# State-space stage of a decoder layer: loops written out, units beyond the last and the empty first accumulation left out

## The chip, the cores and the metric

The kernel runs on one core of one Trainium2 chip. The metric is device microseconds of that core, from launch to end; the lower the better. The five engines (TensorE or PE, VectorE or DVE, ScalarE or ACT, GpSimd or POOL, SyncE or SP) each run their own instruction stream and meet at semaphores.

## The reference, cut to what matters

One decoder layer on x of 16 x 128 x 256: a state-space mixer, then cross attention, then a feed-forward network, each followed by a residual and a layer norm. The change touches the mixer alone:

```python
H, P, N, G, K, CH, E = (32, 128, 128, 8, 4, 32, 256)
proj = x @ in_proj_w.T
gate, hbc, dt = split(proj)
hbc = silu(causal_conv4(hbc) + conv_b)
hs, B, C = split(hbc)                 # B, C: 8 groups, shared by 4 heads each
X = hs.reshape(b, s, H, P) * dt[..., None]
A_cum = cumsum(-exp(A_log) * dt)
y[l] = sum_{m<=l} (C_l . B_m) exp(A_cum_l - A_cum_m) X_m + D * hs_l
h = y * silu(gate)
h = h * rsqrt(mean over 512 channels of h*h + EPS)     # per group of 4 heads
out = (norm_w * h) @ out_proj_w.T
x = layernorm(x + out)
```

## The kernel before

The function decoder_layer calls five stages one after the other, each in a block of its own with a barrier at its end: front (projections of B, C and dt, the products gs of C and B, the cumulative sums), state_space, middle, attention, output. All of them but state_space are plain instruction streams without loops.

The stage state_space works in units of one head and 512 tokens (4 sequences). Four heads that share a norm make a round; four rounds (one for each quarter of the tokens) use the same weight group; there are 8 groups, 32 rounds, 128 units. The stage is a software pipeline written out by hand: in slot m every engine does one part of the units m+3, m+2, m+1 and m.

- PE: x_ps of unit m+3 (L446, project: 6 matmuls of 512 columns), d_ps (L463, L465) and the transpose t_ps (L471) of m+2, y_ps (L481) and gate_ps (L446) of m+1, the output o_ps (L494) of m, and behind a round's last unit the sums of squares ss_ps (L500).
- ACT: first tap of the convolution from x_ps (L525), the exponentials decay (L535), silu of xs (L541), silu of the gate (L547). Exponential and silu each load their table, so two table loads stand in each slot.
- DVE: the other three taps (L603, each waits for the one before), xdt (L611), y (L619), mix (L625).
- POOL: hid = y times the silu of the gate (L659), its square (L666) and the running sum (L670).

At the start of a round's first slot DVE runs finish: var from ss_ps (L585), POOL raises it to the power -0.5 (L649), and four scaled additions bring o_ps into acc (L590). In the slots of each group's last round ACT rounds the next group's weights (L516, w_hi), and DVE scales the output weights (L573, wo) and makes the low part (L576, w_lo). x_ps, gate_ps, t_ps, d_ps, y_ps and o_ps have one buffer each.

Three slots lead in (slot(-1, ...), with Python numbers). The rest are loops on each engine's sequencer: PE and POOL loop over 32 rounds, ACT and DVE over 8 groups with an inner loop of 3 rounds, SP over 8 groups. Heads, tokens and semaphore values are computed in registers; each wait whose value comes from a register is put on an increment of a semaphore named held that nothing waits for. Since the loop bodies are all alike, three things are computed that nobody uses:

- finish(0) adds o_ps and ss_ps, cleared by memsets, before there is anything in them (out_unit and out_used count it);
- the last three slots also work on the units 128, 129 and 130;
- the last round rounds the weights of a ninth group, and SP loads the first group again for it.

Of the kernel before, what the change touches and what calls it, by code (L numbers as in the profile page):

```python
# [17 lines left out]
P = 128  # L18
# [331 lines left out]
def state_space(nc, mem, io):  # L350
# [5 lines left out]


    held = mem["held"]
    xh, xl, gs, cw, cb, dt, ncum, cumT, onehot, mask, acc, dpar, ident, identb = (
        mem[k] for k in ("xh", "xl", "gs", "cw", "cb", "dt", "ncum", "cumT", "onehot", "mask", "acc", "dpar",  # L360
                         "ident", "identb"))
# [8 lines left out]
    def head_of(r, h):  # L370
        return (r // TG) % G * HG + h

    with ExitStack() as ctx:
# [6 lines left out]
        def sem(name):  # L380
            return ctx.enter_context(nc.semaphore(name))

# [17 lines left out]
        x_ps = ps("x_ps", [P, BG, SEQ])  # L400
# [8 lines left out]
        (hi_ready, w_ready, consts, x_ready, tap_ready, chain, conv_done, xs_ready,  # L409
         gate_ready, sg_ready, t_ready, xdt_ready, d_ready, decay_ready, mix_ready, y_ready, yd_ready, hid_ready,  # L410
         sq_ready, sq_chain, out_unit, out_used, var_ready, rms_ready) = (
            sem("ss_" + n) for n in
            ("hi_ready", "w_ready", "consts", "x_ready", "tap_ready", "chain",
             "conv_done", "xs_ready", "gate_ready", "sg_ready", "t_ready", "xdt_ready", "d_ready", "decay_ready",
             "mix_ready", "y_ready", "yd_ready", "hid_ready", "sq_ready", "sq_chain", "out_unit", "out_used", "var_ready",
# [4 lines left out]
        @block.sync  # L420
        def _(sp):
            def load(g):
                cols = bass.ds(g * (HG * P), HG * P)
                for to, of in ((w_raw[:, 0, :, :], io["winT"][:, bass.ds(g * (HG * P) + OFF_X, HG * P)]
                                .rearrange("(k p) c -> p k c", p=P)),
                               (w_raw[:, 1, :, :], io["winT"][:, cols].rearrange("(k p) c -> p k c", p=P)),
                               (wo_raw[:, :, :], io["woutT"][cols, :].rearrange("(h p) e -> p h e", p=P))):
                    sp.dma_start(to, of).then_inc(w_loaded, 16)

            with sp.Fori(0, G) as g:  # L430
                sp.wait_ge(w_ready, g * HG + HG)
                load((g + 1) % G)

        @block.tensor
        def _(pe):
            pe.sem_inc(out_unit, 1)
            pe.wait_ge(consts, 4)

            def project(to, i, n, r, h, ready):

                tok = bass.ds(r % TG * GT, GT)
                pe.wait_ge(w_ready, r // TG * HG + (h + 1))
                pe.sem_inc(held, 1)
                for k in range(KE):
                    for s, (w, x) in enumerate(((w_hi, xh), (w_hi, xl), (w_lo, xh))):
                        mm = pe.matmul(to[:, :, :], w[:, i, k, h * P:(h + 1) * P], x[:, k, tok],  # L446
                                       start=(k == 0 and s == 0), stop=(k == KE - 1 and s == 2))
                mm.then_inc(ready, 1)

            def slot(it, hh, primed):  # L450

                n, r, h = unit(it, hh, 3)
                if primed or n > 0:
                    pe.wait_ge(conv_done, n)
                project(x_ps, 0, n, r, h, x_ready)

                n, r, h = unit(it, hh, 2)
                if primed or n >= 0:

                    if primed or n > 0:  # L460
                        pe.wait_ge(decay_ready, n)
                        pe.sem_inc(held, 1)
                    pe.matmul(d_ps[:, :, :], onehot[:, bass.ds(head_of(r, h), 1), :],  # L463
                              cumT[:, bass.ds(r % TG * GT, GT)], start=True, stop=False)
                    pe.matmul(d_ps[:, :, :], identb[:, :], mask[:, :], start=False, stop=True).then_inc(d_ready, 1)  # L465

                    if primed or n > 0:
                        pe.wait_ge(xdt_ready, n)
# [5 lines left out]
                n, r, h = unit(it, hh, 1)  # L474
                if primed or n >= 0:
                    if primed or n > 0:
                        pe.wait_ge(yd_ready, n)
                    pe.wait_ge(xdt_ready, n + 1)
                    pe.wait_ge(mix_ready, n + 1)
                    for b in range(BG):  # L480
                        mm = pe.matmul(y_ps[:, b, :], xdt[:, h % 2, b, :], mix[:, h % 2, b, :],  # L481
                                       start=True, stop=True)
                    mm.then_inc(y_ready, 1)
                    if primed or n > 0:
                        pe.wait_ge(sg_ready, n)
                    project(gate_ps, 1, n, r, h, gate_ready)

                if primed:
                    n, r, h = unit(it, hh, 0)
                    pe.wait_ge(hid_ready, n + 1)  # L490
                    if h == 0:
                        pe.wait_ge(out_used, it + 1)
                    for b in range(BG):
                        mm = pe.matmul(o_ps[:, b, :], hid[:, h % 2, b, :],  # L494
                                  wo[:, bass.ds(r // TG % 2, 1), h, :].rearrange("p a e -> p (a e)"),
                                  start=(h == 0 and b % 2 == 0), stop=(h == HG - 1), skip_group_check=True)
                    if h == HG - 1:
                        pe.wait_ge(sq_ready, it * HG + HG)
# [3 lines left out]
                    mm.then_inc(out_unit, 1)  # L502

            for hh in range(HG - LEAD, HG):
                slot(-1, hh, False)
            with pe.Fori(0, ROUNDS) as it:
                for hh in range(HG):
                    slot(it, hh, True)

        @block.scalar  # L510
        def _(act):
            def round_weights(g, h):
                act.wait_ge(w_loaded, (g + 1) * (16 * LOADS))
                act.sem_inc(held, 1)
# [4 lines left out]
            def slot(it, hh, primed):  # L519
                n, r, h = unit(it, hh, 3)  # L520
                head = bass.ds(head_of(r, h), 1)

                act.wait_ge(x_ready, n + 1)
                act.sem_inc(held, 1)
                act.activation(xs[:, h, :, :], x_ps[:, :, :], ACT.Identity, bias=cb[:, head],  # L525
                               scale=cw[:, head, TAPS - 1]).then_inc(tap_ready, 1)

                n, r, h = unit(it, hh, 2)
                if primed or n >= 0:
                    if primed or n > 1:  # L530
                        act.wait_ge(mix_ready, n - 1)
                    act.wait_ge(d_ready, n + 1)
                    act.sem_inc(held, 1)
                    for b in range(BG):
                        ex = act.activation(decay[:, h % 2, b, :], d_ps[:, b, :], ACT.Exp,  # L535
                                            bias=ncum[:, bass.ds(r % TG * BG + b, 1), bass.ds(head_of(r, h), 1)])
                    ex.then_inc(decay_ready, 1)

                n, r, h = unit(it, hh, 3)
                act.wait_ge(conv_done, n + 1)  # L540
                act.activation(xs[:, h, :, :], xs[:, h, :, :], ACT.Silu).then_inc(xs_ready, 1)  # L541

                n, r, h = unit(it, hh, 1)
                if primed or n >= 0:

                    act.wait_ge(gate_ready, n + 1)
                    act.activation(sg[:, h % 2, :, :], gate_ps[:, :, :], ACT.Silu).then_inc(sg_ready, 1)  # L547

            for h in range(HG):
                round_weights(0, h)  # L550
            for hh in range(HG - LEAD, HG):
                slot(-1, hh, False)
            with act.Fori(0, G) as g:
                with act.Fori(0, TG - 1) as tg:
                    for hh in range(HG):
                        slot(g * TG + tg, hh, True)
                for hh in range(HG):
                    round_weights(g + 1, hh)
                    slot(g * TG + (TG - 1), hh, True)

        @block.vector
        def _(dve):
            dve.memset(ones[:, :], 1.0).then_inc(consts, 1)
            dve.memset(half[:, :], -0.5).then_inc(consts, 1)
            dve.memset(o_ps[:, :, :], 0.0).then_inc(consts, 1)
            dve.memset(ss_ps[:, :], 0.0).then_inc(consts, 1)
            dve.wait_ge(nw_loaded, 16)

            def rest_of_weights(g, h):
                dve.wait_ge(hi_ready, g * HG + (h + 1))  # L570
                dve.sem_inc(held, 1)

                dve.tensor_tensor(wo[:, bass.ds(g % 2, 1), h, :], wo_raw[:, h:h + 1, :],  # L573
                                  nw[:, bass.ds(g % G * HG + h, 1)].unsqueeze(2).to_broadcast([P, 1, E]), ALU.mult)
# [6 lines left out]
            def finish(it):  # L581

                dve.wait_ge(out_unit, it * HG + 1)
                dve.sem_inc(held, 1)
                dve.tensor_scalar(var[:, :], ss_ps[:, 0:BG], 1.0 / (HG * P), RMS_EPS,  # L585
                                  ALU.mult, ALU.add).then_inc(var_ready, 1)
                dve.wait_ge(rms_ready, it + 1)
                for b in range(BG):
                    to = acc[:, bass.ds((it + (TG - 1)) % TG * BG + b, 1), :].rearrange("p b e -> p (b e)")
# [3 lines left out]
            def slot(it, hh, primed):  # L593
                if primed and hh == 0:
                    finish(it)
                n, r, h = unit(it, hh, 3)
                head = bass.ds(head_of(r, h), 1)
                dve.wait_ge(tap_ready, n + 1)
                for s in range(1, TAPS):
                    if s > 1:  # L600
                        dve.wait_ge(chain, n * 2 + (s - 1))
                    to = xs[:, h, :, s:]
# [1062 lines left out]
```

## Time and profile before

| what | value |
|---|---|
| median of 3 runs | 2147.5 us (2147.41 to 2147.55) |
| profiled execution | 2146.56 us |
| its span, first to last instruction | 2144.8 us |
| PE busy | 1803.8 us, 84% |
| ACT busy | 1665.4 us, 78% |
| DVE busy | 1649.4 us, 77% |
| POOL busy | 580.7 us, 27% |
| mean granted TensorE clock | 0.978 |

Span and busy times are of one profiled execution; the median is of runs without a profile. The stage state_space fills the stretch from about 177 to 1076 us. Matmuls overlap, so that their busy time is no measure of idle time between them: the start times of the weight loads (PEld) say more.

### The profile page before, as it was taken

What the parts mean: (1) busy time and instruction counts of PE and PEld (TensorE: products, weight loads), DVE (VectorE), ACT (ScalarE), POOL (GpSimd) and SP (SyncE); (2) the same over time, 40 slices, a digit from 0 to 9 for tenths busy, and PEclk for the clock granted to TensorE, in tenths of its full rate; (3) what the DMA queues carried; (4) which work ended last, traced back from release to release, by engine and by line L of the source; (5) the groups of instructions that cost most, each with busy time, mean ns of one, the idle gap of its engine ahead of it and who ended that gap; (6) DMA issues with size and microseconds to landing.
All of it is one profiled execution on the core that took longest, in us unless ns stands there. A gap on an engine that the chain in (4) does not pass through costs nothing. (4 is left out here: it accounts for less than half of the span.)

```text
span 2144.8 us, 37991 instructions
## 1 busy us (share of the span) xinstructions
PE 1803.8 (84%) x12364; PEld 1273.8 (59%) x12514; DVE 1649.4 (77%) x2759; ACT 1665.4 (78%) x2987; POOL 580.7 (27%) x482
## 2 busy tenths in 40 slices
PE   6987999999999999999967677777777777774999
PEld 4775878787878787878746333333333333333887
DVE  5886686767686767676888699999999999994443
ACT  4666888888888888888826899999999999994211
POOL 2001555555555555555510000100000100003000
PEclk8998999999999999999989999999999999997999
DMA  4000000000000000000082499999999999995000
GB/s 139 16 6 30 0 30 0 29 0 29 0 29 0 29 0 29 0 26 4 0 182 39 78 182 183 185 184 184 180 185 185 183 183 180 186 186 122 11 11 20
DMA packets 566249, 173.94 MB, mean 81 GB/s; under 512 B 535168, under 2 KB 558592, under 8 KB 566144
## 3 DMA queue, kind: packets, MB, share of 16 engines
q1 hardware_dynamic: 566144, 172.57, 42.8%
q8 instruction: 63, 1.03, 0.2%
q14 instruction: 42, 0.34, 0.1%
HBM read 27.83 MB, written 2.10 MB: 14 GB/s over the span
## 5 line engine op out<-in xcount | busy, mean ns | idle before, releaser
L1223 ACT ACTIVATE levels<-s_ps,nb,qstep 128x512 int16<-128x512 f32 (+1 forms) x768 | 695.8, 915 | 32.7 <-DVE nb L1188 31.7
L1178 DVE TENSOR_REDUCE mx<-s_ps 128x1 f32<-128x512 f32 (+1 forms) x768 | 630.8, 862 | 26.4 <-PE s_ps L1128 26.4
L1128 PE MATMUL s_ps<-kT,qT 128*128 128x512 bf16 x1447 | 445.6, 386 | 200.1 <-ACT levels L1223 181.2
L603 DVE SCALAR_TENSOR_TENSOR xs<-x_ps,cw,xs 128x508 f32<-128x508 f32 (+2 forms) x393 | 291.2, 741 | 174.3 <-ACT xs L525 135.9
L1128 PEld LDWEIGHTS s_ps<-kT,qT 128*128 128x128 bf16 x1532 | 107.8, 97 | 434.8 <-ACT levels L1223 383.7
L659 POOL TENSOR_TENSOR hid<-y,sg 128x512 f32<-128x512 f32 x128 | 175.2, 1369 | 277.7 <-ACT sg L547 185.1
L494 PE MATMUL o_ps<-wo,hid 128*128 x1024 | 242.8, 380 | 4.9 <-DVE acc L590 4.9
L494 PEld LDWEIGHTS o_ps<-wo,hid 128*128 128x128 f32 x1024 | 192.7, 189 | 39.5 <-issue 9.8
L525 ACT ACTIVATE xs<-x_ps,cb,cw 128x512 f32<-128x512 f32 x131 | 101.9, 777 | 116.1 <-PE x_ps L446 116.1
L1246 POOL TENSOR_TENSOR sum_part<-sums 128x16 f32<-128x16 f32 x16 | 3.4, 211 | 689.5 <-ACT levels L1223 689.5
L1136 PEld LDWEIGHTS ao_ps<-vi,levels_T 128*128 128x128 f16 x4096 | 139.9, 96 | 66.9 <-DMA levels_T<-levels 7.6
L535 ACT ACT_TABLE_LOAD x130 | 166.8, 1283 | 2.4
L541 ACT ACT_TABLE_LOAD x130 | 166.8, 1283 | 2.3
L1223 ACT ACTIVATION_READ_ACCUMULATOR levels<-s_ps,nb,qstep 128x1 f32 x768 | 150.6, 196 | 0.0
L535 ACT ACTIVATE decay<-d_ps,ncum 128x128 f32<-128x128 f32 x520 | 148.7, 369 | 1.6
L446 PE MATMUL x_ps<-xh,w_hi 128*128 (+1 forms) x262 | 121.5, 464 | 30.6 <-DVE xs L603 25.7
L1136 PE MATMUL ao_ps<-vi,levels_T 128*128 128x16 f16 x4096 | 140.4, 169 | 7.2 <-DMA levels_T<-levels 7.2
L309 DVE SCALAR_TENSOR_TENSOR bc<-raw_ps,cw,bc 128x1016 f32<-128x1016 f32 (+2 forms) x96 | 119.9, 1265 | 29.9 <-ACT bc L234 27.7
L481 PE MATMUL y_ps<-mix,xdt 128*128 128x128 f32 x1032 | 136.3, 275 | 0.0
L670 POOL TENSOR_TENSOR ssum<-ssum,sq 128x512 f32<-128x512 f32 x96 | 131.3, 1368 | 7.5
L481 PEld LDWEIGHTS y_ps<-mix,xdt 128*128 128x128 f32 x1032 | 125.4, 192 | 0.0
L446 PE MATMUL gate_ps<-xh,w_hi 128*128 (+1 forms) x258 | 112.1, 434 | 0.0
(201 smaller groups left out, 3255.2 us busy)
## 6 DMA issues: line engine op xcount, KB each, us to landing
w_raw<-winT_dram SPq DMA_DIRECT2D x18, 512.0 KB, 4.5
wo_raw<-woutT_dram SPq DMA_DIRECT2D x9, 512.0 KB, 5.7
kT<-zeros SPq DMA_DIRECT2D x4, 1024.0 KB, 18.7
qT<-zeros SPq DMA_DIRECT2D x4, 1024.0 KB, 16.1
levels_T<-levels SPq DMA_TRANSPOSE x256, 4.6
acc<-xT_dram SPq DMA_DIRECT2D x4, 512.0 KB, 5.5
w_bc<-winT_dram SPq DMA_DIRECT2D x16, 128.0 KB, 2.4
acc<-x_dram SPq DMA_DIRECT2D x1, 2048.0 KB, 11.1
```

What stands on the lines that cost most here:

```text
L446: mm = pe.matmul(to[:, :, :], w[:, i, k, h * P:(h + 1) * P], x[:, k, tok], start=(k == 0 and s == 0), stop=(k == KE - 1 and s == 2))
L481: mm = pe.matmul(y_ps[:, b, :], xdt[:, h % 2, b, :], mix[:, h % 2, b, :], start=True, stop=True)
L494: mm = pe.matmul(o_ps[:, b, :], hid[:, h % 2, b, :], wo[:, bass.ds(r // TG % 2, 1), h, :].rearrange("p a e -> p (a e)"), start=(h == 0 and ...
L535: ex = act.activation(decay[:, h % 2, b, :], d_ps[:, b, :], ACT.Exp, bias=ncum[:, bass.ds(r % TG * BG + b, 1), bass.ds(head_of(r, h), 1)])
L541: act.activation(xs[:, h, :, :], xs[:, h, :, :], ACT.Silu).then_inc(xs_ready, 1)
L603: dve.scalar_tensor_tensor(to, x_ps[:, :, 0:SEQ - s], cw[:, head, TAPS - 1 - s], to, ALU.mult, ALU.add).then_inc(chain if s < TAPS - 1 els ...
L659: pool.tensor_tensor(hid[:, hh % 2, :, :], y[:, hh % 2, :, :], sg[:, hh % 2, :, :], ALU.mult).then_inc(hid_ready, 1)
L670: pool.tensor_tensor(ssum[:, :, :], ssum[:, :, :], sq[:, :, :], ALU.add).then_inc(sq_ready, 1)
L1128: return pe.matmul(s_ps[:, BANKS[h % 2][chunk], :], qT[:, qt, h, :], kT[:, h, at:at + GT], start=True, stop=True)
L1136: mm = pe.matmul(o_ps[:, h * HD:(h + 1) * HD], lT[:, s, j, :].bitcast(F16), vi[:, j, h * HD:(h + 1) * HD], start=(j == 0), stop=(j == T // ...
L1178: dve.tensor_reduce(mx[:, u, at:at + 1], src, AX.XY if what == "cd" else AX.X, ALU.max).then_inc(max_done, 1)
L1223: act.activation(levels[:, s, at:at + banks * GT].rearrange("p (c k) -> p c k", c=banks), s_ps[:, bank:bank + banks, :], ACT.Exp, bias=nb[ ...
```

## The change

The loops of state_space become Python loops: each engine has all its instructions one after the other, with constants for heads, tokens and semaphore values, and without held. The slot number m runs from -3 to 127 on PE, ACT and DVE, and a part is written only if its unit lies in 0 to 127. The finish of a round r runs from r = 0, at the start of the next round; the last one behind the last slot. The empty one, the two memsets of o_ps and ss_ps, the ninth group's weights and the reload are gone. The order of each engine's instructions within a slot is as before. x_ps gets a first axis of length 1; buffers are chosen by n % 2 for h % 2, which is the same.

```diff
-    def unit(it, hh, ahead):
-        r = it + (hh + ahead) // HG
-        return r * HG + (hh + ahead) % HG, r, (hh + ahead) % HG
+    UNITS = ROUNDS * HG
+    def place(n):
+        r, h = divmod(n, HG)
+        g, tg = divmod(r, TG)
+        return r, h, g, tg, g * HG + h
...
-            with sp.Fori(0, G) as g:
-                sp.wait_ge(w_ready, g * HG + HG)
-                load((g + 1) % G)
+            for g in range(1, G):
+                load(g)
...
-            pe.sem_inc(out_unit, 1)
-            pe.wait_ge(consts, 4)
...
-                pe.wait_ge(w_ready, r // TG * HG + (h + 1))
-                pe.sem_inc(held, 1)
+                pe.wait_ge(w_ready, head + 1)
...
-            for hh in range(HG - LEAD, HG):
-                slot(-1, hh, False)
-            with pe.Fori(0, ROUNDS) as it:
-                for hh in range(HG):
-                    slot(it, hh, True)
+            for m in range(-LEAD, UNITS):
+                n = m + 3
+                if n < UNITS:
+                    if n >= 1:
+                        pe.wait_ge(conv_done, n - 1 + 1)
+                    project(x_ps[:, n % 1, :, :], 0, n, x_ready)
...
-                    if h == 0:
-                        pe.wait_ge(out_used, it + 1)
+                    if h == 0 and r:
+                        pe.wait_ge(out_used, r)
...
+            for m in range(-LEAD, UNITS):
+                if m >= 0 and m // HG % TG == TG - 1 and m // (HG * TG) + 1 < G:
+                    round_weights(m // (HG * TG) + 1, m % HG)
...
-            dve.memset(o_ps[:, :, :], 0.0).then_inc(consts, 1)
-            dve.memset(ss_ps[:, :], 0.0).then_inc(consts, 1)
...
+                if m > 0 and m % HG == 0:
+                    if m == HG:
+                        dve.wait_ge(acc_loaded, 16)
+                        dve.wait_ge(consts, 2)
+                    finish(m // HG - 1)
...
+            finish(ROUNDS - 1)
...
-            pool.wait_ge(consts, 4)
-            with pool.Fori(0, ROUNDS) as it:
-                factor(it)
+            pool.wait_ge(consts, 2)
+            for n in range(UNITS):
+                r, h, g, tg, head = place(n)
+                if h == 0 and r:
+                    factor(r - 1)
```

## Rows read from the trace of the kernel before

**Rows 1.** Windows: body and tail; busy us (x count) per engine, PE clock, DMA.
```profile
199.00:1041.80 842.80, 815.44 (x4402) 664.95 (x4464) 623.01 (x958) 710.79 (x1147) 456.47 (x372) 1.00 0.04 13
1041.80:1075.80 34.00, 27.09 (x144) 21.37 (x145) 28.87 (x43) 24.89 (x41) 17.44 (x13) 1.00 0.00 0
```
**Rows 2.** Windows: an ordinary round, then a weight group's last round.
```profile
553.40:579.50 26.10, 25.99 (x144) 21.47 (x145) 18.02 (x30) 22.38 (x37) 14.07 (x12) 1.00 0.00 0
605.60:635.35 29.75, 27.13 (x144) 21.40 (x147) 25.81 (x36) 24.23 (x40) 16.44 (x12) 1.00 0.05 13
```
**Rows 3.** Timeline (start, duration in us) of PE's weight loads, ordinary round.
```profile
546.30 0.19 PEld L446 LDWEIGHTS x_ps<-xl,w_hi 128*128 128x128 f32 x1
...
553.48 0.19 PEld L446 LDWEIGHTS x_ps<-xl,w_hi 128*128 128x128 f32 x1
...
559.87 0.19 PEld L446 LDWEIGHTS x_ps<-xl,w_hi 128*128 128x128 f32 x1
...
566.15 0.19 PEld L446 LDWEIGHTS x_ps<-xl,w_hi 128*128 128x128 f32 x1
```
**Rows 4.** Timeline of PE's weight loads, group's last round and after.
```profile
605.76 0.19 PEld L446 LDWEIGHTS x_ps<-xl,w_hi 128*128 128x128 f32 x1
...
611.08 1.59 PEld L494 LDWEIGHTS o_ps<-wo,hid 128*128 128x128 f32 x8 [1.04 <-issue]
...
613.91 0.19 PEld L446 LDWEIGHTS x_ps<-xl,w_hi 128*128 128x128 f32 x1
...
642.79 0.19 PEld L446 LDWEIGHTS x_ps<-xl,w_hi 128*128 128x128 f32 x1
```
**Rows 5.** Timeline of DVE, same round ([idle before <- releaser]).
```profile
609.24 1.66 DVE L590 SCALAR_TENSOR_TENSOR acc<-o_ps,rms,acc 128x256 f32<-128x256 f32 x4 [1.13 <-POOL rms L649]
...
611.72 1.62 DVE L603 SCALAR_TENSOR_TENSOR xs<-x_ps,cw,xs 128x504 f32<-128x504 f32 x2 [0.16 <-DVE xs L603]
613.25 0.68 DVE L611 TENSOR_TENSOR xdt<-t_ps,dt 128x512 f32<-128x512 f32 x1
...
620.40 0.68 DVE L611 TENSOR_TENSOR xdt<-t_ps,dt 128x512 f32<-128x512 f32 x1
```
**Rows 6.** Lines L573, L576, L659: count, min/median/max ns, first and last start.
```profile
L573 DVE TENSOR_TENSOR wo<-wo_raw,norm_w x36: 407/1320/1348, 178.6 to 1065.8; 128x256 f32 x32, 128x256 f32<-128x256 f32 x4
...
L576 DVE TENSOR_TENSOR w_lo<-w_raw,w_hi x36: 679/1522/1525, 179.0 to 1067.0; 128x512 fp32r<-128x512 f32 x36
...
L659 POOL TENSOR_TENSOR hid<-y,sg x128: 1262/1274/1660, 201.4 to 1065.1; 128x512 f32<-128x512 f32 x128
```
**Rows 7.** Timeline, head of the stage; last row from an ordinary round.
```profile
177.29 0.91 DVE L565 MEMSET o_ps<- 128x1024 f32 x1 [0.21 <-issue]
...
178.97 0.68 DVE L576 TENSOR_TENSOR w_lo<-w_raw,w_hi 128x512 fp32r<-128x512 f32 x1
...
179.72 0.29 PEld L446 LDWEIGHTS x_ps<-xh,w_hi 128*128 128x128 f32 x1 [3.89 <-issue]
...
183.58 2.29 DVE L603 SCALAR_TENSOR_TENSOR xs<-x_ps,cw,xs 128x508 f32<-128x508 f32 x3 [1.12 <-ACT xs L525]
...
201.69 1.66 DVE L590 SCALAR_TENSOR_TENSOR acc<-o_ps,rms,acc 128x256 f32 x4 [1.33 <-POOL rms L649]
...
562.80 2.51 DVE L603 SCALAR_TENSOR_TENSOR xs<-x_ps,cw,xs 128x508 f32<-128x508 f32 x3 [1.66 <-ACT xs L525]
```
**Rows 8.** Timeline, tail of the stage.
```profile
1066.80 1.28 ACT L535 ACT_TABLE_LOAD   x1
...
1068.10 1.15 ACT L535 ACTIVATE decay<-d_ps,ncum 128x128 f32<-128x128 f32 x4
...
1074.11 1.66 DVE L590 SCALAR_TENSOR_TENSOR acc<-o_ps,rms,acc 128x256 f32<-128x256 f32 x4 [1.13 <-POOL rms L649]
```
**Rows 9.** Page: a DMA queue; a costliest group (busy, mean ns, idle before, releaser).
```profile
q8 instruction: 63, 1.03, 0.2%
...
L1223 ACT ACTIVATE levels<-s_ps,nb,qstep 128x512 int16<-128x512 f32 (+1 forms) x768 | 695.8, 915 | 32.7 <-DVE nb L1188 31.7
```

More of the change, by code:

```diff
@@ L399, in state_space @@
         rms = sb("rms", [P, BG])
[L400 removed]
+        x_ps = ps("x_ps", [P, 1, BG, SEQ])
         gate_ps = ps("gate_ps", [P, BG, SEQ])
@@ L517, in round_weights @@
                          w_raw[:, :, :, cols].rearrange("p i k c -> p (i k) c")).then_inc(hi_ready, 1)
[L519 to L530, printed above, removed]
+            for h in range(HG):
+                round_weights(0, h)
@@ new lines, in _ @@
+            for m in range(-LEAD, UNITS):
+                if m >= 0 and m // HG % TG == TG - 1 and m // (HG * TG) + 1 < G:
+                    round_weights(m // (HG * TG) + 1, m % HG)
+                n = m + 3
+                if n < UNITS:
+                    r, h, g, tg, head = place(n)
+                    act.wait_ge(x_ready, n + 1)
+                    act.activation(xs[:, h, :, :], x_ps[:, n % 1, :, :], ACT.Identity, bias=cb[:, head:head + 1],
+                                   scale=cw[:, head, TAPS - 1:TAPS]).then_inc(tap_ready, 1)
+                n = m + 2
+                if 0 <= n < UNITS:
+                    r, h, g, tg, head = place(n)
+                    if n > 1:
@@ L531, in slot @@
                         act.wait_ge(mix_ready, n - 1)
                     act.wait_ge(d_ready, n + 1)
-                    act.sem_inc(held, 1)
                     for b in range(BG):
-                        ex = act.activation(decay[:, h % 2, b, :], d_ps[:, b, :], ACT.Exp,
-                                            bias=ncum[:, bass.ds(r % TG * BG + b, 1), bass.ds(head_of(r, h), 1)])
+                        ex = act.activation(decay[:, n % 2, b, :], d_ps[:, b, :], ACT.Exp,
+                                            bias=ncum[:, tg * BG + b, head:head + 1])
@@ L551, in _ @@
[L551 to L559, printed above, removed]
+                n = m + 3
+                if n < UNITS:
+                    act.wait_ge(conv_done, n + 1)
+                    act.activation(xs[:, n % HG, :, :], xs[:, n % HG, :, :], ACT.Silu).then_inc(xs_ready, 1)
@@ L588, in finish @@
                 for b in range(BG):
-                    to = acc[:, bass.ds((it + (TG - 1)) % TG * BG + b, 1), :].rearrange("p b e -> p (b e)")
+                    to = acc[:, r % TG * BG + b, :]
                     ins = dve.scalar_tensor_tensor(to, o_ps[:, b, :], rms[:, b:b + 1], to, ALU.mult, ALU.add)
                 ins.then_inc(out_used, 1)
[L593 to L602, printed above, removed]
-                    dve.scalar_tensor_tensor(to, x_ps[:, :, 0:SEQ - s], cw[:, head, TAPS - 1 - s], to,
-                                             ALU.mult, ALU.add).then_inc(chain if s < TAPS - 1 else conv_done, 1)
-                n, r, h = unit(it, hh, 2)
-                if primed or n >= 0:
-                    if primed or n > 1:
+            dve.memset(ones[:, :], 1.0).then_inc(consts, 1)
@@ new lines, in _ @@
+            dve.memset(half[:, :], -0.5).then_inc(consts, 1)
+            dve.wait_ge(nw_loaded, 16)
+            for h in range(HG):
+                rest_of_weights(0, h)
+            for m in range(-LEAD, UNITS):
+                if m >= 0 and m // HG % TG == TG - 1 and m // (HG * TG) + 1 < G:
+                    rest_of_weights(m // (HG * TG) + 1, m % HG)
+                if m > 0 and m % HG == 0:
[3 more added lines that the diff above has]
+                    finish(m // HG - 1)
+                n = m + 3
+                if n < UNITS:
+                    r, h, g, tg, head = place(n)
+                    dve.wait_ge(tap_ready, n + 1)
+                    for s in range(1, TAPS):
+                        if s > 1:
+                            dve.wait_ge(conv_chain, n * 2 + (s - 1))
+                        to = xs[:, h, :, s:]
+                        dve.scalar_tensor_tensor(to, x_ps[:, n % 1, :, 0:SEQ - s], cw[:, head, TAPS - 1 - s:TAPS - s], to,
+                                                 ALU.mult, ALU.add).then_inc(conv_chain if s < TAPS - 1 else conv_done, 1)
+                n = m + 2
+                if 0 <= n < UNITS:
+                    r, h, g, tg, head = place(n)
+                    if n > 1:
```

178 lines of the change are left out of this document (72 added, 106 removed).

## The prediction

> **What bounds the kernel now.** I read the windows view first. The state-space stage runs from about 177 us to 1076 us, and in its body TensorE is busy 815 of 843 us, at full clock [rows 1]. An ordinary round keeps PE busy 25.99 of 26.10 us while DVE has 18.02; in the last round of a weight group PE has 27.13 of 29.75 and DVE 25.81 [rows 2]. So there are two regimes. Then I read the weight loads in order of time. The second load of x_ps in each slot marks where one slot hands the array to the next. The slots of an ordinary round last 7.18, 6.39 and 6.28 us [rows 3] and again about 6.29: 6.285 is the array's own time, the 7.18 holds the 8 pairs of ss_ps (0.89), and only the 6.39 has 0.11 of idle. Saturated, a round costs 4 x 6.285 + 0.89 = 26.03 us, and no loop, branch or register operation can be seen in it.
>
> Around a weight group's last round it is different: from 605.76 to 642.79, five slots, 37.03 us [rows 4] against 5 x 6.285 + 0.89 = 32.3. There DVE sets the pace: from xdt at 613.25 to the next at 620.40 is 7.15 us of unbroken DVE work [rows 5], because the weights' L573 and L576 take 1.32 and 1.52 us beside POOL, where they can take 0.41 and 0.68 [rows 6]. The excess of the body adds up: 842.8 - 31 x 26.03 = 36 us, of which 7 groups x 4.7 = 33, some 1.8 in ordinary rounds and 1 in the first.
>
> **Head.** Removed are the memsets of o_ps and ss_ps (0.91 and 0.48, from 177.29), ahead of the first weights [rows 7]. L573 could then start when the first w_hi is cast, at about 177.65, for 178.65 now: 1.0 us on the path to the first x_ps. The dropped held increments give about 0.1 in each of three hops, 0.3, and the entry into the loops 0.5 (the third lead slot lasts 6.74, for 6.27 before it). The empty finish (var, POOL's power, four adds, ending 1.66 after 201.69 [rows 7]) holds DVE for 3.1 us ahead of the fourth convolution; PE's slot is 7.23 and would be 6.285: 0.95. Sum 2.75 us.
>
> **Ordinary rounds.** PE's instruction stream is the same, so only the 0.11 goes, in the middle rounds, 16 of them: 1.8 us. The branch, the register operations and held increments are hidden by the queue of matmuls; were that cover gone they would show as the 0.47 below.
>
> **Group-last rounds.** Register operations sit between a wait and the instruction that needed it. The three taps take 2.51 us in the loop and 2.29 where the code is already plain, in the head [rows 7]: 0.22 a slot on DVE. From the end of the taps (611.72 + 1.62 = 613.34) to PE's next x_ps (613.81, a tenth before the row at 613.91) is 0.47 us; in the head, 178.97 + 0.68 = 179.65 to 179.72 is 0.07 [rows 4, 5, 7]. So 0.4 for such a hop. POOL to DVE: 1.33 of waiting for a 1.02 power, where 1.13 is possible when DVE's registers are done ahead [rows 5, 7]: 0.2. The first slot, 8.15 [rows 4], loses two hops (w_hi to L573, taps to x_ps) and the tap gaps: 7.13. Its o_ps, which today waits until 611.08 for the adds that end at 610.90 [rows 4, 5], moves with them. The next two run at 7.15 - 0.22 = 6.93 each. The fourth and fifth together follow DVE through the finish: 6.93, and then 7.15 less the weights' 2.7 plus the finish's 3.0, which is 7.4, less 0.42, 7.0. Sum 7.13 + 6.93 + 6.93 + 13.9 = 34.9 for 37.03, 2.1 to 2.3 us a group, 16 us over 7 groups. What is late next is the same DVE chain, not PE. The bounds: 0 if DVE stays tied to POOL (an L576 of 1.52 ends when POOL lets it), 33 if DVE stops binding; I take the gaps alone, since L573's earlier start meets a hid that takes up to 1.66 for 1.27 [rows 6] and ends no sooner.
>
> **Tail.** From the start of the last round's first slot (1041.8) to the last add (1075.8) are 34.0 us, with PE busy 27.1 [rows 1]. Removed: the whole weights work of that round (DVE and ACT again), x_ps of three units (3 x 1.38), d_ps and t_ps of two, y_ps and gate_ps of one, about 8.6 us of PE, and a reload by SP's queue that nobody waits for. What remains is a chain. With an ordinary first slot (t = 0 at its start) PE is through at 6.3; t_ps of the last unit waits for its silu (6.9); y_ps of unit 126 waits for mix (7.3) and ends at 8.3, gate_ps at 9.7, o_ps at 11.4. ACT loads a table and does four exponentials (1.28 + 1.15 [rows 8]), until 9.8, loads again for the silu of 126: 11.7. Then y_ps and gate_ps of the last unit: 13.7; silu 14.5. POOL works in order: hid(126) 13.0, its square 14.05, its sum 15.35, hid(127) 16.65, square 17.7, sum 19.0. ss_ps after it ends at 19.95, var 20.3, power 21.4, adds (1.66 [rows 8]) 23.1. So 34.0 - 23.2 = 10.8 us. Bounds: 12.5 if ACT's silu of unit 126 needs no table load behind the exponentials; 3 if most of the removed work hides beside this chain (rival d below). I take 10.8, since each link of the chain has a duration in rows of this stage.
>
> **Sum.** 2.75 + 1.8 + 16 + 10.8 = 31.4 us. The profiled execution took 2146.56 us (span 2144.8 and 1.8 around it); it becomes 2115.2, and against the median of 2147.5, 2116. The later stages begin behind a barrier with their own loads and only shift.
>
> **Where straight-line code costs.** The plain program is longer: 68 rows a slot on PE, so some 33 more blocks of 256 on PE's instruction queue and about 28 on the other engines'. Now there are 63 packets on q8, 1.03 MB [rows 9], for 24878 weight loads and matmuls: 97 blocks if each were fetched each time, so the loop's are not fetched again, and its branch costs PE nothing [rows 3]. In the attention stage, plain code with denser rows and busy DMA, ACT's 768 activations at L1223 waited 32.7 us in all, 31.7 of it for DVE [rows 9]: at most 1.0 us is left for fetching.
>
> The Trainium skill (Runtime: NRT & Kernel Launch, Instruction fetch mechanics) says that straight code is fetched ahead and mostly hidden, and that a taken branch out of the two-block window stalls until its block is fetched. On the first point the attention rows agree. By the second the loops' back edges would cost now and their removal bring more than my sum; the 63 packets and the saturated slots around the back edge say that these loops stay in the window.
>
> **Rivals.**
> (a) DVE stays bound to POOL in the group-last rounds and nothing of the 16 comes: 2147.5 - 15.4 = 2132. For it: L576's median is more than twice its shortest time [rows 6]. Against: the tap gaps lie where POOL doesn't matter. 0.13.
> (b) Without register operations the DVE chain meets POOL in a better phase and the weights' operations shorten by 0.7 us a slot: the slots fall to PE's 6.285, all 33 us come, and the time is 2147.5 - 2.75 - 1.8 - 33 - 10.8 = 2099. For it: both have been as short as 0.41 and 0.68 [rows 6]. Against: POOL's three operations need 3.6 to 4.4 us of each slot, so they nearly always meet. 0.09.
> (c) Slower: code supply. Each of some 61 new blocks stalls its engine. Price: q8's 0.2% of 16 engines' span for 63 packets is about 1.1 us a packet [rows 9], so 61 x 1.1 = 67, and 2116 + 67 = 2183. It decides from 0.5 us a block (31.4 / 61). Against: the attention rows. 0.05.
> (d) The tail's work was hidden: it saves 3 instead of 10.8, 2124. It speaks for it that the chain through ACT and POOL remains; against, that in the last slots PE, DVE and ACT all have rows of units that don't exist. 0.08.
>
> **How the numbers follow.** The forecast as such, 2106 to 2126, has 0.65. The range takes in (d) and nearly (a): 2105 to 2131; out of it are (b), (c) and part of (a). A change under 0.2% (4.3 us) can't be told from none. Faster: all but (c) and a remainder of (c)'s small stalls that eat just the gain: 0.93; within 0.2%: 0.02; slower: 0.05.
>
> **What would show it.** DVE's first L576 ending near 178.7; no L590 before the second round; ordinary rounds of 26.0 to 26.1 between x_ps marks; group-last slots of 6.9 us with three taps in 2.3; from the last round's start to the last add about 23 us, with PE waiting for POOL's hid in the last slot; q8 near 96 packets with no gap beside them. Ordinary rounds that lengthen by more than 0.1, or idle time of PE without a releaser, would make it wrong.

## The result, and the profile after

The changed kernel takes 2116.13 us (median of 5 runs, 2112.38 to 2120.53) against 2147.41 us before (5 runs, 2143.91 to 2147.55): ratio 0.9863, 95% interval 0.9845 to 0.9882. The forecast was 2116.0.

I measure the state-space stage from VectorE's memset of ones to the end of its last add to acc. It took 898.79 us (176.98 to 1075.77) and takes 865.12 (177.65 to 1042.77): 33.7 less. The profiled execution as a whole got only 27.0 shorter (2119.57 for 2146.56), so some 6.7 were given back outside this stage (0.7 ahead of it, 6.0 behind); more on that below. I cut the stage at the marks of the prediction, the second x_ps weight load of each slot:

```
                        before    after   change   forecast
first mark               2.91     1.90    -1.0     -1.0
lead (3 slots)          19.24    16.91    -2.3     -0.8
body (31 rounds)       842.82   823.02   -19.8     -18.75
tail                    33.84    23.29   -10.5     -10.8
five slots at a group's end (of the body, 7 times)
                        37.03    34.57   -2.5      -2.1 to -2.3
```

First the windows view of the changed kernel (start:end, length, then busy time and count of PE, PEld, DVE, ACT and POOL, PE's clock, DMA share, GB/s): the body and the tail, which answer to [rows 1], then an ordinary round and a weight group's last round, which answer to [rows 2].

```profile
199.00:1019.40 820.40, 809.84 (x4393) 664.42 (x4453) 622.03 (x950) 708.89 (x1144) 455.81 (x371) 1.00 0.04 12
1019.40:1042.80 23.40, 18.44 (x101) 15.06 (x101) 10.51 (x20) 10.66 (x18) 15.44 (x13) 1.00 0.00 1
...
567.89:593.93 26.04, 25.93 (x144) 21.59 (x146) 18.05 (x29) 22.43 (x38) 14.15 (x12) 1.00 0.00 1
593.93:621.82 27.89, 26.88 (x144) 21.27 (x145) 25.86 (x35) 23.79 (x40) 16.39 (x12) 1.00 0.05 12
```

PE's idle time in the body fell from 27.4 us (842.80 - 815.44) to 10.6. The ordinary round is 26.04 long, the 26.03 of a saturated array. The group's last round went from 29.75 to 27.89 with the same DVE work in it, 25.86: DVE still sets the pace there. The weight loads of PE and DVE's timeline around that round (start, duration) answer to [rows 4, 5]:

```profile
593.93 0.19 PEld L438 LDWEIGHTS x_ps<-xl,w_hi 128*128 128x128 f32 x1
...
600.80 0.19 PEld L438 LDWEIGHTS x_ps<-xl,w_hi 128*128 128x128 f32 x1
...
607.72 0.19 PEld L438 LDWEIGHTS x_ps<-xl,w_hi 128*128 128x128 f32 x1
...
628.49 0.19 PEld L438 LDWEIGHTS x_ps<-xl,w_hi 128*128 128x128 f32 x1
```
```profile
594.54 0.42 DVE L537 TENSOR_TENSOR wo<-wo_raw,norm_w 128x256 f32<-128x256 f32 x1 [1.24 <-ACT w_hi L497]
594.88 0.68 DVE L540 TENSOR_TENSOR w_lo<-w_raw,w_hi 128x512 fp32r<-128x512 f32 x1
...
596.77 1.66 DVE L553 SCALAR_TENSOR_TENSOR acc<-o_ps,rms,acc 128x256 f32<-128x256 f32 x4 [1.13 <-POOL rms L610]
598.35 2.29 DVE L577 SCALAR_TENSOR_TENSOR xs<-x_ps,cw,xs 128x508 f32<-128x508 f32 x3
600.56 0.68 DVE L586 TENSOR_TENSOR xdt<-t_ps,dt 128x512 f32<-128x512 f32 x1
...
601.81 0.68 DVE L601 TENSOR_TENSOR mix<-decay,gs 128x512 f32<-128x512 f32 x1
602.41 1.49 DVE L537 TENSOR_TENSOR wo<-wo_raw,norm_w 128x256 f32<-128x256 f32 x1
603.83 1.52 DVE L540 TENSOR_TENSOR w_lo<-w_raw,w_hi 128x512 fp32r<-128x512 f32 x1
605.28 2.29 DVE L577 SCALAR_TENSOR_TENSOR xs<-x_ps,cw,xs 128x508 f32<-128x508 f32 x3
607.48 0.68 DVE L586 TENSOR_TENSOR xdt<-t_ps,dt 128x512 f32<-128x512 f32 x1
```

From 593.93 to 628.49 are 34.56 us in slots of 6.87, 6.92, 6.92, 7.18 and 6.67. The three taps now stand in one row of 2.29 us. They end at 600.64, and PE's next x_ps follows within 0.16 (mark 600.80); it was 0.57 before (613.34 to the mark at 613.91 [rows 4, 5]). From xdt to xdt DVE takes 6.92 us, still without a gap. The tail's timeline (ACT, POOL and the weight loads) has the chain of the prediction, with POOL near its end and PE waiting for it twice; it answers to [rows 8]:

```profile
1029.21 1.28 ACT L531 ACT_TABLE_LOAD   x1
...
1033.36 0.60 ACT L531 ACTIVATE sg<-gate_ps 128x512 f32<-128x512 f32 x1 [2.26 <-PE gate_ps L438]
...
1034.94 1.26 POOL L619 TENSOR_TENSOR hid<-y,sg 128x512 f32<-128x512 f32 x1
1036.26 1.59 PEld L483 LDWEIGHTS o_ps<-wo,hid 128*128 128x128 f32 x8 [1.61 <-POOL hid L619]
1036.29 1.04 POOL L627 TENSOR_TENSOR sq<-hid 128x512 f32<-128x512 f32 x1
1037.40 1.26 POOL L630 TENSOR_TENSOR ssum<-ssum,sq 128x512 f32<-128x512 f32 x1
...
1038.72 0.97 PEld L488 LDWEIGHTS ss_ps<-ones,ssum 128*128 128x128 f32 x8 [0.87 <-POOL ssum L630]
```

On the page, the queue of instructions and the attention stage's activations answer to [rows 9]:

```profile
q8 instruction: 100, 1.64, 0.3%
...
L1183 ACT ACTIVATE levels<-s_ps,nb,qstep 128x512 int16<-128x512 f32 (+1 forms) x768 | 695.6, 915 | 34.9 <-DVE nb L1148 34.9
```

### The profile page after: what moved, and what is told of

Read it like the earlier page. It is cut to its first block and busy times, and to the rows that moved or that the text cites. A ratio compares the mean times of both kernels' runs of the same rounds, so it can differ in the third digit from the quotient of the medians.

```text
span 2117.8 us, 33475 instructions
## 1 busy us (share of the span) xinstructions
PE 1796.3 (85%) x12321; PEld 1271.0 (60%) x12470; DVE 1629.6 (77%) x2730; ACT 1651.1 (78%) x2964; POOL 578.1 (27%) x481
## 5 line engine op out<-in xcount | busy, mean ns | idle before, releaser
L1183 ACT ACTIVATE levels<-s_ps,nb,qstep 128x512 int16<-128x512 f32 (+1 forms) x768 | 695.6, 915 | 34.9 <-DVE nb L1148 34.9
L577 DVE SCALAR_TENSOR_TENSOR xs<-x_ps,cw,xs 128x508 f32<-128x508 f32 (+2 forms) x384 | 284.6, 741 | 150.7 <-ACT xs L509 141.7
L483 PE MATMUL o_ps<-wo,hid 128*128 128x256 f32 x1024 | 242.3, 379 | 1.2 <-POOL hid L619 1.2
L1183 ACT ACTIVATION_READ_ACCUMULATOR levels<-s_ps,nb,qstep 128x1 f32 x768 | 150.6, 196 | 0.0
L438 PE MATMUL x_ps<-xh,w_hi 128*128 128x512 f32 x256 | 120.1, 469 | 14.6 <-DVE xs L577 10.4
L438 PE MATMUL gate_ps<-xh,w_hi 128*128 128x512 f32 x256 | 111.4, 435 | 0.0
```

Of the source, the lines that this page charges most:

```text
L438: mm = pe.matmul(to, w[:, i, k, h * P:(h + 1) * P], x[:, k, tg * GT:(tg + 1) * GT], start=(k == 0 and s == 0), stop=(k == KE - 1 and s == 2))
L483: mm = pe.matmul(o_ps[:, b, :], hid[:, n % 2, b, :], wo[:, g % 2, h, :], start=(h == 0 and b % 2 == 0), stop=(h == HG - 1), skip_group_che ...
L577: dve.scalar_tensor_tensor(to, x_ps[:, n % 1, :, 0:SEQ - s], cw[:, head, TAPS - 1 - s:TAPS - s], to, ALU.mult, ALU.add).then_inc(conv_chai ...
L1183: act.activation(levels[:, s, at:at + banks * GT].rearrange("p (c k) -> p c k", c=banks), s_ps[:, bank:bank + banks, :], ACT.Exp, bias=nb[ ...
```

## Experiments: the change in pieces

Four kernels were built from the kernel before, each with a part of the change; two more runs are of the changed kernel. All totals are medians of 4 or more runs; "stage" is the profiled execution's.

**Loops written out, nothing else** (`Fori` to `range` on all five engines, all work and the held increments kept):

```diff
-            with dve.Fori(0, G) as g:
-                with dve.Fori(0, TG - 1) as tg:
+            for g in range(G):
+                for tg in range(TG - 1):
-            with pe.Fori(0, ROUNDS) as it:
+            for it in range(ROUNDS):
```

> The kernel before with its loops written out, and nothing else: the increments of held, the memsets, the empty finish, the units 128 to 130 and the ninth weight group all stay. The stage lasted 898.8 us before and 865.1 after the change. My theory (in group-last rounds DVE sets the pace, and the register operations between a wait and its instruction cost 0.22 us a slot on DVE and 0.4 at each hop): the constants take most of it, held leaves about 0.1 a hop; stage 878 us, group-last middle slots 6.93. Rival (the gain is the waits sitting on held, not the registers): stage near 890, slots of 7.1.

Measured: 2123.15 us (2121.76 to 2129.96), ratio 0.9899 [0.9878, 0.9920]; stage 878.38, body 824.55, tail 32.37. The loops alone are 20.4 of the stage's 33.7 us. The held increments stay here, and the taps take 2.29 us all the same: it is the register operations between them that are gone. In the kernel before the source view of the taps' line has them on DVE's sequencer (count, then ns), and in this run it has none:

```profile
L603 DVEq FUSED_REGOPS  x384: 46/64/181, 202.2 to 1070.1; - x192
```

**The same, and no held increments** (`sem_inc(held, 1)` removed on PE, ACT and DVE):

> As the last one, and the increments of held are gone too, so that waits sit on the instructions themselves; all the unused work stays. My theory: stage 875.4 us (865.1 + 8.6 for the tail + 1.7 for memsets and empty finish), the five slots around a group's end 34.6 us as after the change. Rival (the removed work is what brought the gain in the body too): five slots stay near 37.

Measured: 2125.39 us (2125.05 to 2127.99), ratio 0.9903 [0.9886, 0.9919]; stage 876.86. The increments are worth 1.5 us of the stage; the totals can't tell that from nothing. They show in the first slot of a group's last round: 8.15 us before, 7.50 with only DVE's loops written out (below), 7.12 with all loops, 6.87 without the increments as well.

**Only DVE's loops written out** (and DVE's held increments gone):

> The kernel before with DVE's stream alone written out and its increments of held gone; PE, ACT, POOL and SP keep their loops and registers, all unused work stays. My theory: DVE's taps go from 2.51 to 2.29 and its slot in group-last rounds from 7.15 to 6.93; PE keeps its 0.47 behind the taps, so the five slots take about 35.3 instead of 37.0; stage 884 us. Rival (PE's or ACT's loop is what costs): stage 896 or more.

Measured: 2131.57 us (2126.92 to 2132.70), ratio 0.9920 [0.9903, 0.9937]; stage 882.20, body 827.64, a group's five slots 35.19. The windows view of its group-last round, against 29.75 in [rows 2] and 27.89 above:

```profile
598.88:627.16 28.28, 27.03 (x146) 21.29 (x145) 26.04 (x36) 24.18 (x41) 16.35 (x12) 1.00 0.05 11
```

One engine's loops and increments bring 16.6 us. The other four engines' loops and increments bring 5.3 more (882.20 - 876.86, the run before this one), mostly in the groups (35.19 to 34.55 each, 4.5 in all) and in the lead (0.9).

**Loops kept, tail cut** (last round peeled, units beyond the last not computed, no ninth weight group):

```diff
-            with pe.Fori(0, ROUNDS) as it:
+            with pe.Fori(0, ROUNDS - 1) as it:
                 for hh in range(HG):
                     slot(it, hh, True)
+            for hh in range(HG):
+                slot(ROUNDS - 1, hh, True, last=True)
```

> The kernel before with its loops, but the last round stands behind them without the units 128 to 130, without the ninth group's weights and the reload. Empty finish and memsets stay. My theory (tail 33.8 to 23.3 us after the change, little of it by constants): stage 888 us, tail 23.5. Rival (the cut work was hidden behind the chain through ACT and POOL, and it is the constants that shortened the tail): stage 896, tail 31.

Measured: 2136.17 us (2133.19 to 2137.99), ratio 0.9952 [0.9935, 0.9968]; stage 886.22, tail 23.50 for 33.84, body 840.67. The tail is its own 10.3 us, whatever the loops do. The body got 2.1 us shorter too, though its loops are kept: 0.3 us in each group's five slots. No run says why.

**The changed kernel again**, on the chip of the experiments below:

> The kernel of the change as it is, on the same chip as the next three, for a time beside theirs. It took 2116 us (2112.4 to 2120.5) before. In its profile the state-space stage was 33.7 us shorter, but all that follows took 6 us longer (middle stage 134.1 for 131.0, attention 738.8 for 736.8, output 202.1 for 201.2). If that is chance of where the clock's cold stretches fall, the stage is again 865.1 and the rest between 1066 and 1075; if the change itself causes it, the rest is 1075 again.

Measured: 2116.31 us (2114.83 to 2117.17), ratio 0.9860 [0.9845, 0.9875]; stage 866.06 with a lead of 18.19. The lead of 16.91 above is thus not the change's alone. The windows view of 178 to 198 us shows what differs, first the kernel before, then after, then this run:

```profile
178.00:198.00 20.00, 13.01 (x42) 9.05 (x44) 11.84 (x21) 10.34 (x18) 0.00 (x0) 0.57 0.25 79
```
```profile
178.00:198.00 20.00, 13.53 (x50) 9.08 (x52) 13.42 (x22) 12.93 (x22) 0.00 (x0) 0.83 0.24 79
```
```profile
178.00:198.00 20.00, 14.21 (x48) 9.95 (x49) 13.30 (x22) 12.79 (x22) 0.00 (x0) 0.74 0.23 79
```

The granted clock (third from the right) was 0.57, 0.83 and 0.74 of full speed there, means of stretches at half (1.2 GHz) and at full speed (2.4 GHz); in the kernel before PE had its half speed from 178.3 to 195.3 without a break. Two executions of the same program differ by 1.3 us in the lead with it.

**The head put back into the changed kernel**:

```diff
+            dve.memset(o_ps[:, :, :], 0.0).then_inc(consts, 1)
+            dve.memset(ss_ps[:, :], 0.0).then_inc(consts, 1)
...
-                if m > 0 and m % HG == 0:
+                if m >= 0 and m % HG == 0:
                     finish(m // HG - 1)
```

> The kernel after, with the head of the kernel before put back: VectorE clears o_ps and ss_ps (two memsets, 1.0 us), TensorE waits for all four memsets, and the empty first accumulation (1 us) runs before unit 0; all else stays straight code with the tail cut. My theory (head = 1.0 for the first weight load, then about 1 us for the empty accumulation in the first round): the stage grows from the 865.1 to 866.1 us of the changed kernel to 867 to 868, the first x_ps mark from 1.9 to 2.9 us, body and tail stay at 822.8 and 23.3; the whole about 2118. Rival 1 (the lead shrank for another reason, the clock of TensorE, and the empty accumulation hides): the stage grows by 1.0 only. A second question: attention takes 736.4 us in all kernels built from the one before and 738 in all built from the one after. If o_ps being cleared or the pace of the head decides it, it is back at 736.4 here; if it is something else in the changed text, it stays at 738.

Measured: 2117.67 us (2114.11 to 2119.65), ratio 0.9861 [0.9841, 0.9881]; stage 868.08, so 2.0 more than the changed kernel run again: first mark 2.95 for 1.91, lead 18.34 for 18.19, first slot of the first round 6.99 for 6.26. The empty accumulation is on the path here: the taps start at 202.75, as its adds end, and PE's next x_ps waits for them. How much it costs depends on the execution: 0.73 beside this 6.26, 0.46 beside the 6.52 to 6.53 of the other profiles with the changed head, while the run with all loops written out and held kept has the accumulation too and a slot of 6.39. So rival 1 falls in its second half; its first half, that the clock shortened the lead, is what the 18.34 shows, for here PE was at half speed from 178.2 to 195.3 as in the kernel before. The total can't be told from the changed kernel's. The attention part took 737.10, between the two values of the second question.

## Experiments: what still binds the group-last rounds

The changed kernel keeps 34.56 us where the array alone needs 32.3. The first two runs ask why w_lo and wo take 1.52 and 1.49 us there, the last two go on from the faster version.

**GpSimd's squares and sums cut to one column in these rounds** (the rest of the sum of squares is left out there, so the scale of those rounds is another):

```diff
+                some = slice(0, 1) if tg == TG - 1 and r < ROUNDS - 1 else slice(0, SEQ)
-                pool.tensor_tensor(sq[:, :, :], hid[:, n % 2, :, :], hid[:, n % 2, :, :], ALU.mult).then_inc(sq_chain, 1)
+                pool.tensor_tensor(sq[:, :, some], hid[:, n % 2, :, some], hid[:, n % 2, :, some], ALU.mult).then_inc(sq_chain, 1)
...
```

> The kernel after, with the squares and their sum on GpSimd cut to one column of 128 in the group-last rounds (left out there: the rest of the sum of squares, so the scale of those rounds is another). Theory of contention (two-input operations on VectorE run at a third of their speed only while GpSimd streams operands): the scaling of the output weights falls from 1.32 us towards the 0.4 us of the head, w_lo from 1.52 towards 0.69, so up to 1.7 us less in each of 28 slots; with GpSimd's y x sg left (1.27 us of each slot), about half of it comes, the groups fall from 34.6 to about 31 us and the stage from 865 to some 840 to 850. Rival (these operations are long in this place for another reason, such as TensorE's or ScalarE's reads of the same weights): they keep 1.3 and 1.5 us and the stage stays at 865 within 1.

Measured: 2102.64 us (one run, beside 2147.57); stage 853.48, groups 32.89. DVE's code is that of the changed kernel. The source view of L540 in this run (count, min/median/max ns, first and last start), then DVE's and POOL's timelines in its group-last round:

```profile
L540 DVE TENSOR_TENSOR w_lo<-w_raw,w_hi x32: 677/679/687, 178.6 to 925.1; 128x512 fp32r<-128x512 f32 x32
```
```profile
596.78 0.69 DVE L601 TENSOR_TENSOR mix<-decay,gs 128x512 f32<-128x512 f32 x1
597.38 1.49 DVE L537 TENSOR_TENSOR wo<-wo_raw,norm_w 128x256 f32<-128x256 f32 x1
598.80 0.68 DVE L540 TENSOR_TENSOR w_lo<-w_raw,w_hi 128x512 fp32r<-128x512 f32 x1
```
```profile
596.94 1.65 POOL L619 TENSOR_TENSOR hid<-y,sg 128x512 f32<-128x512 f32 x1 [2.85 <-DVE y L594]
```

In the changed kernel the source view of the same line is

```profile
L540 DVE TENSOR_TENSOR w_lo<-w_raw,w_hi x32: 682/1523/1525, 178.6 to 936.8; 128x512 fp32r<-128x512 f32 x32
```

With POOL's square cut short, every w_lo takes 0.68; the 0.84 was contention, the rival falls. The stage did not come down to the 840 to 850 of the expectation: the slots behind the first are 6.28, 6.29, 7.18 and 6.28, PE's own time, and the groups can't go under its 32.3. wo keeps its 1.49 in this place because hid stays: POOL's hid (596.94 to 598.59) ends, and wo ends 0.28 later. It is a handover, not a slower rate: mix keeps hid back (1.65 for 1.28 us), hid keeps wo back, and in the changed kernel the square (603.70 to 604.80) keeps w_lo back until 0.55 us before its end.

The Trainium skill (SBUF — State Buffer, Who interferes with whom) says that a DVE instruction with two inputs in SBUF and a GpSimd instruction that reads SBUF take turns for whole instructions, whichever came first, while one with at most one SBUF input, outside the two-port modes, is not touched. The traces agree on both sides: wo, w_lo and mix have two such inputs, and the taps and xdt, with one in PSUM, kept 2.29 and 0.68 beside the same POOL work.

**wo scaled a round or two earlier**, in rounds where DVE has 8 us to spare:

```diff
+            early = {(1, 2): 0, (1, 3): 1, (2, 2): 2, (2, 3): 3}
             for m in range(-LEAD, UNITS):
+                if m >= 0 and m // (HG * TG) + 1 < G and (m // HG % TG, m % HG) in early:
+                    scale_out(m // (HG * TG) + 1, early[m // HG % TG, m % HG])
```

> The change, with the scaling of the next group's output weights (wo) taken out of the group's last round and spread over four slots of its second and third rounds. My theory (DVE sets the pace of a group's last round, 6.93 us a slot for PE's 6.285): without its 1.3 us DVE's slot is 5.6 and PE sets the pace; the five slots 34.57 become 32.6, stage 865.1 - 7 x 2.0 = 851 us. Rival (the low part w_lo meets POOL at another phase and fills what was freed): slots stay at 6.9, stage 865.

Measured: 2101.45 us (2098.60 to 2104.17), ratio 0.9789 [0.9776, 0.9802]; stage 851.23, groups 32.55. The windows view of the group-last round that starts at 588.33, then of its body; and the source view of L537:

```profile
588.33:614.60 26.27, 26.27 (x146) 21.51 (x145) 22.93 (x33) 24.44 (x41) 15.49 (x12) 1.00 0.11 38
197.00:1005.80 808.80, 808.75 (x4465) 668.50 (x4464) 603.04 (x953) 710.75 (x1147) 446.64 (x371) 1.00 0.04 13
```
```profile
L537 DVE TENSOR_TENSOR wo<-wo_raw,norm_w x32: 415/418/424, 178.0 to 894.5; 128x256 f32<-128x256 f32 x32
```

PE is busy through the whole body, 808.75 of 808.80; of the five slots only the first, 6.53, is still over the array's own time. Where wo now stands it takes 0.42 each time. In total this version beats the changed kernel on the same chip by 14.9 us (2116.31 - 2101.45), as the stage does, by 14.8 (866.06 - 851.23): 14.1 in the seven groups, the rest in the head, where the first mark comes at 1.44 for 1.91.

**PE kept working between the stages** (10 matmuls into PSUM that nobody reads behind the state-space stage, 32 at the start of the next):

```diff
+            for _ in range(10):
+                pe.matmul(gate_ps[:, 0, :], ident[:, :], ident[:, :], start=True, stop=True)
...
+            for _ in range(32):
+                pe.matmul(x_ps[:, 0, 0:P], ident[:, :], ident[:, :], start=True, stop=True)
```

> The change, with 10 matmuls of ident by ident on PE behind the last ss_ps and 32 more at the start of the middle stage, about 2 and 7 us, where PE otherwise idles until the middle stage's weights have landed. Their results are overwritten. Theory (what the middle stage lost is cold clock after this idle stretch): the 13.7 us at the lower clock behind the stage's end shrink and the middle stage falls from 134 to about 128 us, total 3 to 6 us faster than the change. Rival (the middle stage waits for DMAs and DVE, the clock does not matter): no difference.

Measured: 2113.57 us (2109.15 to 2116.65), ratio 0.9838 [0.9825, 0.9852], which overlaps the changed kernel's 0.9845 to 0.9875. The 20 us behind the stage, first the changed kernel run again, then this one:

```profile
1043.10:1063.10 20.00, 11.60 (x31) 7.27 (x32) 12.23 (x41) 2.05 (x3) 5.26 (x5) 0.69 0.99 243
```
```profile
1043.10:1063.10 20.00, 17.97 (x96) 13.22 (x96) 14.68 (x45) 2.75 (x4) 5.26 (x5) 1.00 0.96 249
```

And the 20 us after those, in the same order:

```profile
1063.10:1083.10 20.00, 14.88 (x109) 11.27 (x108) 19.41 (x28) 8.75 (x11) 0.00 (x0) 1.00 1.13 191
1063.10:1083.10 20.00, 16.41 (x106) 13.03 (x107) 19.41 (x28) 7.84 (x9) 0.00 (x0) 0.83 1.12 196
```

The mean granted clock went from 0.69, a stretch at 1.2 GHz ahead of one at 2.4, to 1.00 in the first 20 us, with PE at work up to their start, but from 1.00 to 0.83 in the next 20: the stretch at 1.2 GHz came later and was half as long (1063.8 to 1070.6 for 1042.0 to 1055.6); it did not go away. The stage that begins there took 131.16 us for 130.93. It starts with the DMA engines 96 to 99% busy, and that, not the clock, is the likelier limit there; no gain is shown.

**All together** (wo early, PE kept working, and the last two units' squares and sums on DVE, idle in the tail, instead of POOL):

> The last two together, and the squares and sums of the last two units on DVE instead of POOL (POOL's order, hid, square, sum, hid, square, sum, ends the tail: 23.3 us from the last round's start). Theory: tail about 21, stage 849, in all 2116 - 14 - 2 - 4 = 2096 us. Rival for the tail (ACT's silu of the last gate ends it): tail stays 23.

Measured: 2099.03 us (2094.98 to 2100.41), ratio 0.9779 [0.9766, 0.9793]; stage 849.70, tail 21.71 for 23.28. It is the fastest by its median, but its interval overlaps that of wo early alone (0.9776 to 0.9802). In its tail POOL no longer waits for itself but for ACT's last silu, behind PE's gate_ps:

```profile
1018.05 1.26 POOL L634 TENSOR_TENSOR hid<-y,sg 128x512 f32<-128x512 f32 x1 [1.58 <-ACT sg L533]
```

## Why the prediction held, step by step

**Head, 2.75 forecast.** The memsets: 1.0, and 1.0 measured (2.91 to 1.90; with them put back, 2.95). The empty accumulation: 0.95 forecast, 0.46 to 0.73 by the run that puts it back. Hops and loop entry: 0.8 forecast; the lead fell from 19.24 to 18.33 with loops and held increments gone and to 18.34 with the head put back, 0.9, in two runs whose clock was at half speed as long as before. That makes 2.4 to 2.6. The profiled execution of the changed kernel shows 4.0 (1.0 + 2.3 + 0.7); what it has more came with a mean clock of 0.83 for 0.57, which the prediction did not have.

**Ordinary rounds, 1.8 forecast.** 26.04 for 26.10 where I looked, but not every round had the same idle. As a remainder: 19.8 for the body, less 17.6 for the groups and 0.7 for the first slot, leaves 1.5. The step held.

**Group-last rounds, 16 forecast, 17.6 measured** (2.46 in six of the groups and 2.77 in the first, whose five slots took 37.33). The taps lost 0.22 a slot and the hop from taps to x_ps lost 0.4, as worked out. POOL to DVE went from 1.33 to 1.13 at the finish in the fifth slot; at the one in the first slot it was 1.13 before [rows 5]. The slots were forecast as 7.13, 6.93, 6.93 and 13.9; they are 6.87, 6.92, 6.92 and 13.85. The first slot is what was mis-sized: it lost 1.28 us and not 1.02. The forecast slots give 34.9, so 2.13 a group and 14.9 in all; the 16 took the upper end of 2.1 to 2.3, and that came nearer by chance. That DVE's chain stays the limit was right: wo grew from 1.34 to 1.49 us, since it starts earlier and still ends behind hid, so that written-out code gained nothing there, as the prediction had it. Written out on DVE alone, a group gave 1.84 of the 2.46.

**Tail, 10.8 forecast, 10.5 measured.** From the stage's mark at 1019.48, the forecast ends of hid(126), hid(127), its sum and the last add were 13.0, 16.65, 19.0 and 23.1; they are 13.04, 16.72, 19.18 and 23.29. The table load behind the exponentials, which the upper bound of 12.5 had left out, is there (1029.21). Rival (d) is out: the cut tail alone gave 10.3.

**Outside the stage, 0 forecast.** Here the prediction was wrong, by an amount that the spread of the runs (8.1 us for the changed kernel) covers. In the profiled execution of the changed kernel the three later parts took 3.0, 2.0 and 0.9 us more than before (134.05 for 131.01, 738.83 for 736.79, 202.14 for 201.20). The first and last vary with the execution: run again, the same program has 130.93 and 201.59, and over all twelve profiles the middle part runs from 129.9 to 134.8. The attention part is 736.3 to 736.8 in the kernel before and the four built from it, 737.1 with the head put back, and 737.6 to 738.8 in the other profiled versions of the changed kernel. The excess is idle time of ACT before L1183, 34.9 for 32.7, and most of it is made by DVE: at five of the 256 bias operations (L1148, numbers 11, 32, 199, 220 and 241, counted from 0) DVE starts 0.49 to 0.50 us after its last maximum, and 0.14 elsewhere. Operations 10 and 11 in the timeline of the changed kernel run again:

```profile
1203.04 0.22 DVE L1148 CUSTOM_DVE_ANT_0 low<-mx,shift,nstep 128x3 f32<-128x3 f32 x1
1203.19 0.09 DVE L1148 DVE_READ_ACCUMULATOR2_ANT nb<- 128x1 f32 x1
1203.19 2.42 DVE L1138 TENSOR_REDUCE mx<-s_ps 128x1 f32<-128x512 f32 x3
1206.11 0.22 DVE L1148 CUSTOM_DVE_ANT_0 low<-mx,shift,nstep 128x3 f32<-128x3 f32 x1 [0.50 <-DVE mx L1138]
```

That is 5 x 0.35 = 1.75 us. The same five stand in the other profile of the changed kernel and in those of its variants, one operation earlier each in the last version, which gives DVE more to do ahead of them; none is in the kernel before, the four built from it or the run with the head. (The 0.6 us that the first changed execution and the run with the head have beyond this come in one wait near the start of the attention.) Places that stand 21 operations apart (11 and 32; 199, 220 and 241) and move with DVE's instruction stream speak for the supply of DVE's instructions; no run tests that.

So the step that the later stages only shift failed by 0.8 to 2.0 us in the attention part (737.6 to 738.8 for 736.8), and the match of 2116.0 with 2116.13 is in part luck: in the two profiled executions the stage gave 2.3 and 1.3 us more than 31.4, and the other parts gave back 6.7 and 1.8.

**The rivals.** (a) is out: the groups did shrink though w_lo stayed at 1.52. (b) had the right mechanism for the rest, contention with POOL, but its condition didn't arise by itself: the weights' operations are short only in a group's first slot (0.42 and 0.68 at 594.54), and there they were so before (0.43 and 0.68 at 607.01). When wo was moved away, nearly all of the (b) gain came, 14.8 us on top. (c), slower by code supply, is out at its price: q8 fetched 100 packets where I had 96, and the written-out loops won 20.4 us with 101. But its refutation had a gap: I counted ACT's 31.7 us of waiting for DVE as no fetching, and it would hold DVE's own. If the five late operations above are such, code supply cost 1.75 us. By the Trainium skill's second point (Runtime: NRT & Kernel Launch, Instruction fetch mechanics), a taken branch out of the fetched window stalls. No run shows such a stall in the loops: with DVE's written out q8 stays at its 63 packets and the profile's other queue of instructions, q14, goes from 42 to 50, and the ordinary round was saturated in both forms.

## What to carry to other kernels

Before unrolling, ask on which engine the chain is unbroken: there each register operation between a wait and its instruction is paid, here 0.22 us a slot on DVE and 0.4 in a hop to PE, while on an engine with queued work it costs nothing. Then look at two-input SBUF operations of DVE that meet GpSimd's: moving one of them into rounds with slack was worth 14.1 us in those rounds, nearly as much as the loops of DVE. And measure a gain in the stage where it arises: the parts behind it differed by 4.3 us between two executions of the same program.

## What was not expected of the hardware

- GpSimd and DVE hand over by whole instructions: a 128x256 product of 0.42 us took 1.49, a 128x512 difference of 0.68 took 1.52, and up to 1.76 when it came to stand behind hid.
- Halving the stretch at 1.2 GHz at the start of the middle stage, 13.6 to 6.8 us, brought nothing that can be measured there (130.93 and 131.16 us), with the DMA engines 96 to 99% busy in its first 20 us.
- In the attention part, DVE started five of 256 like operations 0.35 us late in the changed kernel, at the same places in both its profiles, and none in the kernel before.
